# Context attention with heads of 32: the order of second products, sums of probabilities and the middle side job

## The reference, cut to what matters

```python
H, D, C1, C2 = (16, 32, 128, 64)
xn = _ln(x, lnx_g, lnx_b)            # [16, 256, 128]
yn = _ln(y, lny_g, lny_b)            # context, [16, 1601, 64]
q = jnp.einsum('bsc,hcd->bhsd', xn, wq)
k = jnp.einsum('btc,hcd->bhtd', yn, wk)
v = jnp.einsum('btc,hcd->bhtd', yn, wv)
a = jax.nn.softmax(jnp.einsum('bhsd,bhtd->bhst', q, k) * D ** (-0.5), axis=-1)
o = jnp.einsum('bhst,bhtd->bhsd', a, v)
x_out = x + o.transpose(0, 2, 1, 3).reshape(...) @ li1_w + li1_b
```

## Time and profile before

| | |
|---|---|
| time, median of 3 runs | 7738.05 us (7690.1 to 7750.57) |
| span of the profiled execution | 7680.6 us |
| PE busy | 6854.6 us, 89% |
| PEld busy | 3108.2 us, 40% |
| DVE busy | 5897.9 us, 77% |
| ACT busy | 4972.7 us, 65% |
| POOL busy | 2316.8 us, 30% |

### The profile page before, as it was taken

The page is one execution under the profiler, slowest core; times in us unless marked ns, Lnnn a source line. Parts: engine busy times, 40 slices in busy tenths (PEclk is TensorE's granted clock), DMA queues, the critical chain, the costliest instruction groups (busy, mean ns, idle before and its releaser), DMA issues. The chain is left out here.

```text
span 7680.6 us, 186325 instructions
## 1 busy us (share of the span) xinstructions
PE 6854.6 (89%) x73814; PEld 3108.2 (40%) x73814; DVE 5897.9 (77%) x12885; ACT 4972.7 (65%) x9846; POOL 2316.8 (30%) x2368
## 2 busy tenths in 40 slices
PE   6999999977999998788769999999996889999979
PEld 2333333343333333344424444444444433333335
DVE  6888888846898997788757777777774488999955
ACT  4787788834888886455446666666653168888842
POOL 1222222111211210155435555555554112212100
PEclk9999999987999999899879999999998589999989
DMA  5344444104434341100100000000001144343400
GB/s 101 86 98 94 94 91 94 44 27 84 95 78 103 81 92 44 28 18 17 40 22 10 9 8 10 6 10 9 5 5 56 28 103 99 75 103 85 85 26 12
DMA packets 319830, 417.82 MB, mean 54 GB/s; under 512 B 56533, under 2 KB 238054, under 8 KB 318969
## 3 DMA queue, kind: packets, MB, share of 16 engines
q1 hardware_dynamic: 317432, 405.36, 23.2%
q10 hardware_dynamic: 1536, 0.53, 0.0%
HBM read 225.41 MB, written 174.66 MB: 52 GB/s over the span
## 5 line engine op out<-in xcount | busy, mean ns | idle before, releaser
L688 ACT ACTIVATE a_probs<-scores_ps 128x512 f32<-128x512 f32 (+2 forms) x5248 | 2821.1, 591 | 356.9 <-PE scores_ps L608 263.7
L747 DVE TENSOR_REDUCE a_unit_max<-bank 128x1 f32<-128x512 f32 x3072 | 2003.7, 683 | 180.2 <-PE bank L595 145.3
L625 PE MATMUL bank<-a_probs,a_v_sb 128*9 128x256 f32 (+1 forms) x20992 | 1615.8, 380 | 29.3 <-ACT a_out_sb L695 20.3
L1299 ACT ACTIVATE cross_probs<-scores_ps 128x512 f32<-128x512 f32 (+1 forms) x1792 | 868.6, 571 | 590.4 <-PE scores_ps L1194 590.4
L608 PE MATMUL scores_ps<-a_stack 64*128 64x256 bf16 (+1 forms) x10496 | 1131.7, 275 | 60.9 <-ACT a_probs L688 55.9
L1381 DVE TENSOR_REDUCE cross_unit_max<-bank 128x1 f32<-128x512 f32 x1536 | 979.2, 685 | 253.3 <-PE bank L1180 250.2
L747 DVE TENSOR_REDUCE a_unit_max<-scores_ps 128x1 f32<-128x512 f32 x1536 | 1049.8, 683 | 160.4 <-PE scores_ps L595 143.1
L595 PE MATMUL bank<-a_stack 63*128 63x512 bf16 (+2 forms) x3413 | 1039.7, 372 | 7.4 <-DMA a_stack<-a_stack_dram 2.1
L1465 POOL TENSOR_TENSOR cross_added<-cross_probs 128x1024 f32<-128x1024 f32 x384 | 905.6, 2358 | 327.3 <-PE bank L1227 241.5
L608 PEld LDWEIGHTS scores_ps<-a_stack 64*128 64x128 bf16 (+1 forms) x10496 | 373.3, 96 | 991.1 <-ACT a_probs L688 831.7
L512 POOL CAST a_parts<-a_qk 128x512 bf16<-128x512 f32 (+3 forms) x225 | 117.7, 523 | 1893.8 <-ACT a_qk L707 1814.2
(11 more groups left out here) (421 smaller groups left out, 10031.3 us busy)
## 6 DMA issues: line engine op xcount, KB each, us to landing
a_stack_dram<-a_parts SPq DMA_DIRECT2D x288, 400.2 KB, 4.3
a_stack<-a_stack_dram SPq DMA_DIRECT2D x256, 348.2 KB, 8.0
a_stack<-a_stack_dram SPq DMA_DIRECT2D x128, 444.2 KB, 9.9
a_ctxT<-in_ctxT SPq DMA_DIRECT2D x48, 400.2 KB, 4.8
a_stack_dram<-a_parts SPq DMA_DIRECT2D x288, 64.0 KB, 2.4
a_stack_dram<-a_parts SPq DMA_DIRECT2D x96, 128.0 KB, 2.4
f_x<-x_after_dram SPq DMA_DIRECT2D x32, 256.0 KB, 3.3
x_after_dram<-a_res SPq DMA_DIRECT2D x48, 128.0 KB, 4.3
```

Source lines behind the costliest of these rows:

```text
L625: ins = pe.matmul(out_bank[32 * h:32 * h + V8, q0:TOK], v[0:n, e.t, 4 * e.g + h, :], A.probs[0:n, held, o + q0:o + TOK], start=(e.t == 0), ...
L688: act.activation(by_pair(A.probs[0:n, b, a * 512:(a + 1) * 512])[:, :, q0:TOK], by_pair(score_bank[(2 * e.i + a) % 3][0:n, :])[:, :, q0:TO ...
L747: ins = dve.tensor_reduce(unit_max[:, e.g % 2, qt, 2 * a + j, c:c + 1], bank[:, 0:e.s.chunks[c][1]], AX.X, ALU.max)
L1299: act.activation(probs[0:n, b, h, 0:m, :].rearrange("p m q -> p (m q)"), score_bank[h][0:n, 0:m * TOK], ACT.Exp, scale=scale).then_inc(S[" ...
```

## The change

For the stage over the context (`own` is false) the units of part 1 and the side job of slot 1 now come behind `sums`, and also behind `take` and `norm` where there are any. For the self-attention the order is as it was.

```diff
@@ segment32 @@
         if pv:
             plan.append(Ev("pv", s=s, g=steps[k][0], j=steps[k][1], i=zero + k))
-        plan += by_part[1] + at.get((i, 1), [])
+        if s.own:
+            plan += by_part[1] + at.get((i, 1), [])
         if pv:
             plan.append(Ev("sums", s=s, g=steps[k][0], j=steps[k][1], i=zero + k))
             if steps[k][1] == per_quad - 1:
...
                 norm = [Ev("norm", g=steps[k][0], i=zero + k)]
                 if not s.own:
                     plan += norm
+        if not s.own:
+            plan += by_part[1] + at.get((i, 1), [])
         plan += by_part[2]
```

## The result

| | before | changed |
|---|---|---|
| time, median of 11 runs each | 7707.51 us (7685.33 to 7750.57) | 7757.41 us (7725.92 to 7797.91) |
| ratio | | 1.0059, 95% interval 1.0031 to 1.0086 |
| span of the profiled execution | 7680.6 us | 7755.7 us |
| the stage over the context, first to last exponential | 1880.7 us | 1937.4 us |

The changed kernel is slower by 0.6%, some 50 us by the medians and 24 to 66 us by the interval. The forecast was +51 us. So I go by the stage, not by the spans.

The account below looks back on a forecast made before the run. PE's instruction stream was taken to set the pace; the terms summed to +3.3 us per batch element, rounded down to 3.2, times 16 = +51 us, so 7738 + 51 = 7789 us, range 7757 to 7818.

Parts of the forecast that it names:

- Shape changes, 0.13 us where nothing else waits: In 25 of 28 steps `pv` and sums come together; where nothing else waits, a step gets 0.13 us shorter.
- +0.44 at ten steps: Places 0, 3 and 4: `k` or `v` starts 0.44 us later, scores still await DVE's copy; +4.4 us per batch element.
- `turn`, +0.35, three times of four: Place 6: sums no longer cover ACT's copy, scores 0.35 us later, one of four hidden; +1.0 us per batch element.
- `q`, -0.3 for the four: Steps with a `q` job: -0.13 us each, POOL's later cast hidden; -0.3 us for the four, statistics falling in one.
- a first unit of place 6 that waits for POOL's cast: Sign that would show the forecast wrong: at place 6 the first unit waits for POOL's cast, expected 0.44 us later but hidden.
- The quad's end, -1.7: Places 1 and 2: earlier reductions save 0.2 us twice, `ctx` quads 0.65 each; -1.7 us per batch element.
- the bank of that copy is wanted only after the norm anyway: Quad's end: copy of `v` behind the norm not holding PE up; otherwise places 1 and 2 longer by up to 0.69 less 0.13.
- POOL, zero: POOL's adding: sums come 0.5 to 1.1 us earlier, which fits its spare time and releases nothing PE awaits; zero.
- fewer drains: Rival: only shape changes count, copies are no wait; -70 us, 7668 us, chance 0.07.
- slack: Rival: delays of places 3, 4 and 0 vanish in PE's waits for reductions; within 20 us of 7738, chance 0.15.
- a loss at the quad's end: Rival: `take` and `norm` ahead of the copies hold banks up to 2.1 us more; +117 us, 7855 us, chance 0.12.

Follow-up runs that it names:

- experiment 2: Kernel before, with the new order only at places 1 and 2 (the end of a quad); ratio 0.9989, 0.9958 to 1.002.
- version 7: Kernel before, new order only at places 1, 2, 5 and the last `v`, quad's end as `take`, `v` job, `norm`; 7653.9 us against 7726.49, ratio 0.9919.
- experiment 1: Kernel before, with the new order only at places 0, 3 and 4, without the last `v`; ratio 1.0088, 1.0053 to 1.0124.
- doubled copy: Changed kernel, with DVE copying each half of `k` jobs and of `v` jobs at place 3 twice; 7893.7 us in one run.
- experiment 3: Kernel before, with the new order only at place 6, where the `turn` job stands; ratio 1.0031, 0.9996 to 1.0065.
- experiment 4: Kernel before, with the new order only at places 1, 2, 5 and the step of the last `v`; ratio 0.997, 0.994 to 1.0001.

## Why the prediction was right, point by point

1. *Shape changes, 0.13 us where nothing else waits.* Right where it could be seen: 0.17 at the last `v`, of which 0.03 came with the quad's end (experiment 2), and 0.13 over places 5 and 6 together (step 12 and 13 of version 7: 7.26 instead of 7.39). Twenty of the 25 steps had something else that waits. The rule of the Trainium skill that a change of the tiling mode drains TensorE ("TensorEngine Tiling (Array Packing)", Key Properties) is borne out: the step with a `v` job had three gaps in the weight loads before, 0.41, 0.76 and 0.41 us, and has two now, 0.41 and 0.76, with none between `pv` and the sums. But as a forecast for this change it would have had the wrong sign.

2. *+0.44 at ten steps.* 0.43 in eight of them and 0.39 in a ninth (step 17, 4.60 to 4.99). The tenth is step 7, at place 0 behind the layer-norm statistics, 4.71 to 4.75 in the changed kernel. In experiment 1 both of these have their 0.43 as well (4.60 to 5.03, 4.71 to 5.14). In the changed kernel 0.04 of step 17's is taken off by the quad's end before it, and step 7's is hidden by the delay that it took over from place 6. The doubled copy shows that these steps hang on the copy.

3. *`turn`, +0.35, three times of four.* 0.39 alone: the scores start 0.12 us behind the end of ACT's copy, where I had put 0.07. In the changed kernel it is 0.28 for place 6, since 0.11 of the 0.13 of `q` is taken off there. In step 6 it was +0.44, and step 7, which had its own 0.43 from the copy, grew by only 0.04: the statistics did absorb it.

4. *`q`, -0.3 for the four.* It was some -0.4: -0.13 to -0.15 over places 5 and 6 in three quads, +0.03 in the quad with the statistics, for which I had counted nothing. I had named a first unit of place 6 that waits for POOL's cast as a sign that I was wrong. It does wait, 47 times for 16.5 us by the waits view above, so this sign came true. The timeline at place 6 shows why it cost nothing:

```profile
4626.32 1.29 DVE L1384 TENSOR_REDUCE cross_unit_max<-bank 128x1 f32<-128x512 f32 x2 [0.46 <-PE bank L1183]
...
4626.89 0.32 PEld L1183 LDWEIGHTS bank<-cross_qk_b 32*128 32x128 bf16 x2 [0.35 <-POOL cross_qk_b L1483]
```

The two units' loads start at 4626.89 and 4627.12. The second goes into a bank that the first of the two reductions frees at 4627.01, so an earlier cast would not have let it start sooner. The engine stood only 0.14 us between the two loads; by that, a cast later by more than 0.14 us would have cost time.

5. *The quad's end, -1.7.* 0.20, 0.20, 0.69 and 0.57 in the trace make -1.66. For the quads with `ctx` my terms, 0.64 - 0.12 + 0.2, add up to 0.72 and not to the 0.65 that I wrote; the 0.65 is nearer to what was measured. The copy of `v` behind the norm ate what I said; experiment 7 shows the price of that place, 0.33 us a quad. I had held that the bank of that copy is wanted only after the norm anyway; in two quads of four PE did stand 0.41 us for it.

6. *POOL, zero.* In the changed kernel's waits view no wait of the sums for POOL appears. In that of the kernel before there were 46, 7.7 us in all, at place 6.

The sum was +3.2 us per batch element, and the medians say 121.8 - 118.5 = +3.3, or 52 us for sixteen. The stage grew by 56.7: two elements ran at a clock of 0.99 in the changed kernel and at 1.00 before and grew by some 1.5 us more than the rest, and the last two grew by 4.2 and 4.3 (the last at 0.98). The mechanism was right term by term, but that the sum is so close is in part luck, since small misses cancel: by experiments 1, 3, 2 and 4 the copies cost 4.3 (4.4 forecast), `turn` 1.2 (1.0), the quad's end brings 1.8 (1.7), and `q` with the last `v` 0.5 (0.43). The time itself was less well met. I forecast 7789 us, and it is 7757.41, only just inside my range of 7757 to 7818: the three runs that I started from had a median of 7738.05, the eleven have one of 7707.51.

The rivals fell: fewer drains by experiments 1 and 3, slack by the nine steps that kept their delay, a loss at the quad's end by experiment 2.

## What to carry to other kernels

An instruction that seems to cost PE time may be what covers a copy: before it is moved, look at what the instruction behind it waits for, and how long ago that began. In a fixed order the best place of an independent piece of work differs from step to step, and a change for all steps at once adds up gains and losses that can be told apart in the timeline of a single period. Where two engines share one event (`take` on ACT and `norm` on DVE), each engine's own order is worth a look: putting them apart by one event took 0.33 us more off every quad.

## What the runs showed of the hardware that I had not expected

The self-attention stage with the same order of instructions took 491.7 us from first to last exponential in one execution and 509.9 in another. The mean granted clocks of the windows around it were 0.93 and 0.89. These 18 us are a third of what this change moved. What decides the clock from one execution to the next stays open.
